# A four-layer graph network: node sums by (tile, block) visits held in PSUM, and waits by the group needed

## The reference

```python
# 1: two attention convolutions (with self loops): g = h @ W
e = leaky_relu(s[src] + d[dst]); alpha = softmax of e over the edges of dst
h = segment_sum(g[src] * alpha, dst) + bias
# 2: GCN (with self loops): dis = rsqrt(deg)
out = segment_sum((x @ W)[src] * dis[src] * edge_weight * dis[dst], dst) + b
# 3: relational attention, with a time mask sigmoid((t[dst] - edge_time) / |coeff|), 8 heads
out = segment_sum(v * attn, dst)
# 4: GGN: agg = segment_sum((h @ W_msg)[src], dst); a GRU cell of agg and h; @ W_out
x = layernorm(x + layer(x))          # after each of the four
```

## Time and profile before

| | us |
|---|---|
| median of three runs | 6013.23 (6009.44 to 6026.37) |
| profiled execution | 6018.44 |
| its span, first to last instruction | 6016.5 |
| busy: PE, PEld, DVE, ACT, POOL | 3699.8, 3070.5, 3610.2, 1531.2, 4144.0 |

### The profile page before, as it was taken

One profiled execution on the slowest core, in us unless ns is written; L12 is line 12 of the kernel. 1 busy time (PEld: TensorE's weight loads), 2 busy tenths in 40 slices (PEclk: granted clock), 3 DMA queues, 4 the chain that ended last, 5 costly groups with the idle time before them and its releaser, 6 DMA issues. The chain is left out here.

```text
span 6016.5 us, 106908 instructions
## 1 busy us (share of the span) xinstructions
PE 3699.8 (61%) x29332; PEld 3070.5 (51%) x29332; DVE 3610.2 (60%) x10962; ACT 1531.2 (25%) x3918; POOL 4144.0 (69%) x4416
## 2 busy tenths in 40 slices
PE   4765355566364344445555799999975864444556
PEld 2555355455353333445554577777754753344444
DVE  4699475699573235444554788888869952223235
ACT  0476000377100011000000455555540140000004
POOL 6677777377777746777776577777773447777772
PEclk8655698655596555555555899999987985555557
DMA  5687576488585544566772466666663732221221
GB/s 164 179 242 229 159 247 214 132 242 241 160 247 173 151 122 139 165 175 183 189 197 55 142 207 206 206 207 207 207 148 113 205 85 53 53 53 51 53 53 37
DMA packets 564739, 946.34 MB, mean 157 GB/s; under 512 B 122022, under 2 KB 225983, under 8 KB 563599
## 3 DMA queue, kind: packets, MB, share of 16 engines
q0 software_dynamic: 140576, 316.92, 21.1%
q1 hardware_dynamic: 263907, 405.95, 21.0%
q10 hardware_dynamic: 159712, 216.63, 11.7%
HBM read 705.34 MB, written 235.74 MB: 156 GB/s over the span
## 5 line engine op out<-in xcount | busy, mean ns | idle before, releaser
L256 POOL DMA_INDIRECT s_rows<-rel_tab,src_v x832 | 809.6, 973 | 272.5 <-issue 246.7
L256 POOL DMA_INDIRECT stash<-gat_tab,src_g x784 | 780.6, 996 | 251.8 <-issue 238.0
L256 POOL DMA_INDIRECT gcn_rows<-gcn_tab,src_g x784 | 751.9, 959 | 247.9 <-issue 236.2
L256 POOL DMA_INDIRECT ggn_rows<-ggn_tab,src_g x784 | 747.7, 954 | 248.3 <-issue 248.0
L256 POOL DMA_INDIRECT stash<-in_x,src_g x736 | 738.9, 1004 | 236.9 <-issue 223.1
L1595 PE MATMUL e_psb<-tmp,e_oh 128*128 x3328 | 553.4, 328 | 554.9 <-DVE e_oh L1566 459.3
L1595 PEld LDWEIGHTS e_psb<-tmp,e_oh 128*128 128x128 f32 x3328 | 495.7, 231 | 612.9 <-issue 612.8
L2108 PE MATMUL gcn_pso<-gcn_rows,gcn_oh 128*128 x1952 | 500.9, 438 | 484.1 <-SPq L965 396.4
L1940 PE MATMUL ggn_pso<-ggn_rows,ggn_oh 128*128 x1952 | 470.0, 417 | 492.2 <-SPq L965 486.1
L2108 PEld LDWEIGHTS gcn_pso<-gcn_rows,gcn_oh 128*128 128x128 f32 x1952 | 431.2, 325 | 510.2 <-issue 510.2
L1940 PEld LDWEIGHTS ggn_pso<-ggn_rows,ggn_oh 128*128 128x128 f32 x1952 | 405.8, 308 | 557.0 <-issue 557.0
(11 more groups left out here) (502 smaller groups left out, 8071.9 us busy)
## 6 DMA issues: line engine op xcount, KB each, us to landing
edge_v<-stash SPq DMA_DIRECT2D x392, 256.0 KB, 2.2
g_lo_rows<-lo_rows ACTq DMA_DIRECT2D x392, 256.0 KB
e_values<-edge_v SPq DMA_DIRECT2D x392, 256.0 KB, 4.2
oh_dram<-tmp ACTq DMA_DIRECT2D x208, 256.0 KB
s_oh<-oh_dram SPq DMA_DIRECT2D x208, 256.0 KB
edge_v<-acc SPq DMA_DIRECT2D x208, 256.0 KB
r_values<-edge_v SPq DMA_DIRECT2D x208, 256.0 KB, 3.0
tmp<-drel_rows ACTq DMA_DIRECT2D x208, 128.0 KB
```

The lines of the kernel that those rows point to most:

```text
L256: pool.indirect_dma_start(rows[:, t, :], None, tab[:, :], bass.IndirectOffsetOnAxis(ap=edges[:, t:t + 1], axis=0)).then_inc(s_land, 16)
```

## The change

Visits by (group, block) and all their tables are gone (`edge_rows`, `dst_tab`, `w_tab`, `grp_row`, `blk_row`, `slot_row`, `done_row`, L408 and the chain to `gvi`). `grow` is loaded straight from the inputs by nine DMAs, and half of the weight loads move from ACT's to SP's queue, ahead of the kept stores. GCN and GGN use the 832 (tile, block) visits in 208 iterations; sums stay in PSUM (four banks in GCN, eight in GGN), preset with `acc` by PE (identity matmul) for the first blocks and by ACT for later ones, and taken out by ACT. POOL itself announces landed groups, each behind the gathers of the next group; there are 16 slots. A new row `need_row` holds for each iteration the number of groups that must be there; PE waits for that count in GCN, GGN and `gat_sums`. In `gat_sums` DVE builds one-hots ten iterations ahead of the weighted values, with a ring of 14. In GGN the four one-hots of an iteration are one TENSOR_TENSOR instead of four TENSOR_SCALAR. In GCN the one-hots stay four TENSOR_SCALAR (from `drel_v` and `tm_v`), the DMAs of the static part move from ACT to SP, DVE instead of ACT takes the time products out of PSUM, and the three additions and Tanh come after the last iteration.

```diff
-V = GROUPS + BLOCKS - 1
...
-SLOTS = 14
+LEAD = 10
+AHEAD = LEAD + 4
+FEW = 4
...
-                    for a, name in enumerate(("dst", "src", "edge_type_64", "edge_weight")):
-                        arr = A[name] if a < 3 else A[name].bitcast(I32)
-                        sp.dma_start(edge_rows[0:FULL, a * GE:(a + 1) * GE],
...
+                    sp.wait_ge(s_pad, 3)
+                    for a, arr in enumerate((A["dst"], A["src"], A["edge_weight"].bitcast(I32))):
+                        sp.dma_start(grow[:, 0, a, :], arr[0:HALF_G * GE].rearrange("(g e) -> g e", e=GE)).then_inc(s_dl, 16)
+                        sp.dma_start(grow[0:FULL - HALF_G, 1, a, :], arr[HALF_G * GE:FULL * GE].rearrange("(g e) -> g e", e=GE)).then_inc(s_dl, 16)
+                        sp.dma_start(grow[FULL - HALF_G:HALF_G, 1, a, 0:REST], row(arr[FULL * GE:E])).then_inc(s_dl, 16)
+                    for g in range(EARLY, KEPT_FIRST):
+                        edges_of(g)
...
-                    sp.dma_start(grow[:, :, :], edge_rows[:, :].rearrange("(c p) e -> p c e", c=2)).then_inc(s_dl, 16)
-                    for g in range(EARLY, KEPT_FIRST):
-                        edges_of(g)
+                    weights(sp, later)
...
-                    for g in range(EARLY):
-                        gather_early(g)
-                    pool.wait_ge(s_gv, 1)
-                    for c in range(VC):
-                        pool.indirect_dma_start(er[:, c, :, :].rearrange("p a e -> p (a e)"), None, edge_rows[:, :],
-                                                bass.IndirectOffsetOnAxis(ap=gvi[:, c:c + 1], axis=0)).then_inc(s_er, 16)
-                    for g in range(EARLY, KEPT_FIRST):
+                    for g in range(KEPT_FIRST):
                         gather_early(g)
...
+                    link(v.tensor_scalar(need_row[:, :].unsqueeze(2), tile_i[:, :].rearrange("o (n t) -> o n t", t=GT)[:, :, GT - 1:GT], 2, None, ALU.arith_shift_right))
+                    link(v.tensor_scalar(need_row[:, :], need_row[:, :], 1, None, ALU.add))
...
-        def gather_rows(pool, rows, tab, s_row, s_used):
+        def ring_gathers(pool, rows, tab, s_row, s_in, s_o):
+            def came(g):
+                pool.wait_ge(s_row[g % WSLOTS], (g // WSLOTS + 1) * (16 * GT))
+                pool.sem_inc(s_in, 1)
             for g in range(GROUPS):
-                k = g % SLOTS
-                if g >= SLOTS:
-                    n = pool.value_load(done_row[0:1, g - SLOTS:g - SLOTS + 1], min_val=1, max_val=V)
-                    pool.wait_ge(s_used, n + RING)
+                if g >= WSLOTS:
+                    pool.wait_ge(s_o, GT * (g - 3))
                 pool.sem_inc(s_turn, 1)
-                gather_group(pool, rows[:, k, :, :], tab, src_g[:, g * GT:(g + 1) * GT], s_row[k])
-        def announce(sp, s_row, s_landed):
-            for g in range(GROUPS):
-                sp.wait_ge(s_row[g % SLOTS], (g // SLOTS + 1) * (16 * GT))
-                sp.sem_inc(s_landed, 1)
+                k = g % WSLOTS
+                gather_group(pool, rows[:, k * GT:(k + 1) * GT, :], tab, src_g[:, g * GT:(g + 1) * GT], s_row[k])
+                if g >= 1:
+                    came(g - 1)
+            came(GROUPS - 1)
+        def preset(act, ps_b, count, b, s_ev):
+            nc.scalar.activation(ps_b[:, b % count, 0:D], acc[:, b * D:(b + 1) * D], ACT.Copy).then_inc(s_ev, 1)
+        def evict(act, ps_b, count, b, s_o, s_tk, s_ev):
+            n = act.value_load(ends_row[0:1, b:b + 1], min_val=1, max_val=VT)
+            act.wait_ge(s_o, n)
+            nc.scalar.activation(acc[:, b * D:(b + 1) * D], ps_b[:, b % count, 0:D], ACT.Copy).then_inc(s_tk, 1)
+            if b + count < BLOCKS:
+                act.wait_ge(s_tk, b + 1)
+                preset(act, ps_b, count, b + count, s_ev)
+        def ring_sums(pe, ps_b, count, bank_of, oh, rows, s_in, s_oh, s_ev, s_o, beside=None):
+            its = count // GT
+            for b in range(count):
+                nc.tensor.matmul(ps_b[:, b, 0:D], ident[:, :], acc[:, b * D:(b + 1) * D], start=True, stop=True).then_inc(s_ev, 1)
+            for n in range(ITERS):
+                if n % its == 0:
+                    here = slice(n * GT, (n + its) * GT)
+                    blocks = several(mybir.EngineType.PE, blkv_row[0:1, here], BLOCKS - 1) if beside is not None else None
+                    newest = pe.value_load(blkv_row[0:1, here.stop - 1:here.stop], min_val=0, max_val=BLOCKS - 1)
+                    banks = several(mybir.EngineType.PE, bank_of[0:1, here], count - 1)
+                    slots = several(mybir.EngineType.PE, wslot_row[0:1, here], WSLOTS * GT - 1)
+                need = pe.value_load(need_row[0:1, n:n + 1], min_val=1, max_val=GROUPS)
+                pe.wait_ge(s_oh, n + 1)
+                if n % its == 0:
+                    pe.wait_ge(s_ev, newest + 1)
+                pe.wait_ge(s_in, need)
+                for t in range(GT):
+                    bank, slot = banks[n % its * GT + t], slots[n % its * GT + t]
+                    nc.tensor.matmul(ps_b[:, bass.ds(bank, 1), 0:D].rearrange("p o d -> p (o d)"), oh[:, n % RING, t, :],
+                                     rows[:, bass.ds(slot, 1), :].rearrange("p o d -> p (o d)"),
+                                     start=False, stop=True, skip_group_check=True).then_inc(s_o, 1)
+                if beside is not None:
+                    beside(n, blocks)
...
-                        def step(i, k):
-                            n = i * WSLOTS + k
-                            if n >= RING:
-                                dve.wait_ge(s_o, i * (WSLOTS * GT) + (k + 1 - RING) * GT)
-                            if n < GROUPS:
-                                dve.wait_ge(s_val[k % LOADED], i * (WSLOTS // LOADED * 16) + (k // LOADED + 1) * 16)
-                                w = gx[:, :, bass.ds(n * GT, GT)]
-                                v.tensor_copy(wv4[:, k, :, D:WCOLS], w.rearrange("p h t -> p t h"))
-                                v.tensor_tensor(wv4[:, k, :, 0:D], vr[:, k % LOADED, :, :], w[:, 0, :].unsqueeze(2).to_broadcast([P, GT, D]), ALU.mult)
-                            v.tensor_tensor(oh[:, k % RING, :, :], iota[:, :].unsqueeze(1).to_broadcast([P, GT, P]),
-                                            drel_v[:, bass.ds(n * GT, GT)].unsqueeze(2).to_broadcast([P, GT, P]), ALU.is_equal).then_inc(s_wv, 1)
+                        def weighted(g):
+                            if g >= WSLOTS:
+                                dve.wait_ge(s_o, GT * (g - 3))
+                            k = g % WSLOTS
+                            dve.wait_ge(s_val[g % LOADED], g // LOADED * 16 + 16)
+                            w = gx[:, :, g * GT:(g + 1) * GT]
+                            v.tensor_copy(wv4[:, k, :, D:WCOLS], w.rearrange("p h t -> p t h"))
+                            v.tensor_tensor(wv4[:, k, :, 0:D], vr[:, g % LOADED, :, :], w[:, 0, :].unsqueeze(2).to_broadcast([P, GT, D]), ALU.mult).then_inc(s_wv, 1)
+                        def onehots(n):
+                            if n >= AHEAD:
+                                dve.wait_ge(s_o, GT * (n + 1 - AHEAD))
+                            v.tensor_tensor(oh[:, n % AHEAD, :, :], iota[:, :].unsqueeze(1).to_broadcast([P, GT, P]),
+                                            drel_v[:, n * GT:(n + 1) * GT].unsqueeze(2).to_broadcast([P, GT, P]), ALU.is_equal).then_inc(s_oh, 1)
...
-                        for k in range(WSLOTS):
-                            step(0, k)
-                        for i in range(1, GROUPS // WSLOTS):
-                            for k in range(WSLOTS):
-                                step(i, k)
-                        for k in range(WSLOTS):
-                            step(GROUPS // WSLOTS, k)
+                        for n in range(LEAD):
+                            onehots(n)
+                        for g in range(GROUPS):
+                            weighted(g)
+                            if g + LEAD < ITERS:
+                                onehots(g + LEAD)
+                        for n in range(GROUPS + LEAD, ITERS):
+                            onehots(n)
...
+                            need = pe.value_load(need_row[0:1, n:n + 1], min_val=1, max_val=GROUPS)
+                            pe.wait_ge(s_oh, n + 1)
+                            if n % 2 == 0:
+                                pe.wait_ge(s_ev, newest + 1)
+                            pe.wait_ge(s_wv, need)
...
-                                i = v_.tensor_scalar(oh[:, k % 2, t, :], iota[:, :], dst_tab[:, col_], None, ALU.is_equal)
+                        v.memset(acc[:, :], 0.0).then_inc(s_z, 1)
+                        for n in range(ITERS):
+                            if n >= RING:
+                                dve.wait_ge(s_o, (n + 1 - RING) * GT)
+                            v.tensor_tensor(oh[:, n % RING, :, :], iota[:, :].unsqueeze(1).to_broadcast([P, GT, P]),
```

(24 more changed lines are left out.)

447 lines of the change are left out of this document (125 added, 322 removed).

## The result

The changed kernel takes 6253.76 us (median of four runs, 6242.55 to 6255.64) against 6014.9 us, a ratio of 1.0391 with a 95% interval of 1.0371 to 1.0410: slower by 239 us. 6046 us was forecast. The direction was right and the size was not; the range ended at 6072.

A forecast was written before the change was run, and what follows sets the result against it. POOL's indirect gathers, one every 1.25 us, were taken as the bound. 6018.4 - 15 (preparation) - 28 (attention sums) + 2 (GCN body) + 7 (GCN end) + 67 (GGN body) = 6051.4, 6046 us for the median; range 5980 to 6072.

The forecast's parts named there:

- What bounds the kernel: Whole kernel: POOL's row of indirect gathers bounds it, one starting every 1.25 us, 4960 of 6016.5 us; PE waits for gathers.
- Sums of both attention layers: Ends of both attention layers: need_row leaves two or three iterations behind the last weights, not 13; -28 us (-34 to -20).
- PE's clock or load being the bound after all: Rival on the visits: their rework shows by itself because PE is the bound; chance under 0.05, not priced apart.
- GGN body: GGN's one-hots: each TENSOR_TENSOR starts 0.20 us ahead of a group's fourth gather, stretching it 0.35 us; +67 us (45 to 85).
- Preparation: First phase: dropping the gvi chain and two gathers ends it at 76 us, with a 5 us stall; -15 us (-19 to -7).
- GCN body: GCN's iterations and POOL's landing waits: nearly all lies beside 5.0 us per group; +2 us (0 to 10).
- GCN end: Behind GCN's last iteration: additions, table load and Tanh no longer run beside gathers; +7 us (5 to 9).
- POOL would not starve on landings: GCN: landing waits cost nothing within a group's 5.0 us; the rival, POOL starving, had +30 us, 6076 us, chance 0.06.
- Sum: Whole kernel: all terms added to the profiled run give 6051.4 us, or 6046 us for the median.

The follow-up runs named there:

- e9: Changed kernel, but in the attention sums PE loads need_row only from iteration 160 on and waits for the constant n + 1 before: 6095.5 us.
- e14: Kernel of e9 with GGN's TENSOR_TENSOR one-hot 0.85 us earlier, in a ring of five buffers: 6044.8 us (1.0045).
- e13: Changed kernel with need_row loaded from iteration 160 on, GGN's one-hots as four TENSOR_SCALAR, and nothing large ahead of the stores on SP's preparation queue: 6022.8 us (1.0018).
- e15: Changed kernel, but in the attention sums PE loads one need_row value for two iterations, that of the later one: 6150.9 us (1.0231).
- e10: Changed kernel with need_row from iteration 160 on, a MEMSET before each GGN one-hot, edge numbers ahead of grow, weight loads back on ACT: 6097.5 us.
- e1: Changed kernel, but in the attention sums PE waits for the constant min(n + 1, 196), without need_row loads: 7992.0 us against 7947.7 for the kernel before.
- e2: The kernel of e9 on a chip where the kernel before takes 7947.7 us: 8016.6 us (1.0081).

## Why the prediction was right or wrong

**What bounds the kernel.** The 5.0 us for each group was right for GCN and GGN and was carried to the attention sums without a look at a stretch there. The earlier trace rows show only GCN and GGN. The same view at 820 to 920 us, quoted above, has the clock at 0.95 and weighted groups 1.8 us apart. On that row hangs the larger part of the error, 170 of the 208 us between 6046 and 6253.8; most of the rest is the preparation, 31.

**Sums of both attention layers** (forecast -28). This is the step that failed. It weighed the wait's meaning (a group needed earlier) and the one-hots, and gave the register load that carries the wait no term at all. The load stands on PE's sequencer 416 times, of which some 180 in the first and 120 in the second layer are iterations that PE works off without waiting for gathers. It lengthened such an iteration by 0.75 us, 0.2 of them idle time of PE and 0.55 the loss of the upper clock. The gain itself was there: in e9, with the load from iteration 160 on, the four stretches of both layers add to 2181.8 us against 2205.8 before, -24. Four iterations were left behind the last weights, not two or three. In the changed kernel only the second layer shows it (the finishing operations 20.8 us behind the last gather, not 34.5), as the first layer's PE is behind until its end (44.1 us). The list of rivals had "PE's clock or load being the bound after all" at under 0.05, argued from the earlier trace rows again.

**GGN body** (forecast +67, measured +54, range 45 to 85). Right, mechanism and place: the fourth gather of a group (mean 1206 ns, the other three 946 to 990) is held up by the one-hot, and e14 removes it by moving the one-hot. The held gathers add to 49 us; some 6 more are a gather of 7.8 us at the stage's start. Of the chain, one link was off: from the group's end to PE's weight load it takes 1.88 us (median of 160 groups; 1.93 in the group below), not 1.73, with POOL instead of SP passing the landing on.

```profile
5503.67 0.94 POOL L250 DMA_INDIRECT ggn_rows<-ggn_tab,src_g  x1 [0.30 <-issue]
...
5506.54 1.78 PEld L899 LDWEIGHTS ggn_psb<-ggn_rows,ggn_oh 128*128 128x128 f32 x8 [3.22 <-issue]
```

So the distance was 0.05 us in the median and not 0.20, at the very edge: 110 gathers were held up, 100 of them fourth ones of the 196 groups, by 0.48 us in the median, instead of nearly every fourth one by 0.35. The product came out near the forecast partly by luck. The Trainium skill infers on its page "SBUF — State Buffer", section "Who interferes with whom", that a tensor_tensor leaves the writing of DMA descriptors alone. The inference doesn't hold here: with the TENSOR_TENSOR 0.06 us ahead, the gather takes 1.45 us. The rule of the Trainium skill's same section that a tensor_tensor with both inputs in SBUF contends with GpSimd's reads would fit, as the gather takes its row numbers (src_g) from SBUF; no run tells the two apart. The Trainium skill says there too that a tensor_scalar in a 2-port mode blocks GpSimd. With four TENSOR_SCALAR the fourth gathers have a mean of 951 ns (e13, without one of 7.1 us) and none but that one is over 1.02 us; in which mode these ran, no view tells. That the later one waits until the earlier ends, which the same section says, agrees with the held gathers, which end at a fixed 0.81 to 0.83 us behind the one-hot.

**Preparation** (forecast -15, measured +16). The term named the right queue and sized it wrongly. It counted nine loads of grow at about 0.5 us of issue each. Two of them, small ones of 0.6 KB, held SP for 22.5 and 15.2 us, each behind two of 196 and 194 KB:

```profile
8.06 22.50 SPq L321 DMA_DIRECT2D grow<-in_src  x1
...
32.74 15.20 SPq L321 DMA_DIRECT2D grow<-in_edge_weight  x1
47.98 11.94 SPq L313 DMA_DIRECT2D p_early_edges<-in_src  x7
```

So not only the store of group 0 came late, as forecast, but the edge numbers of group 5, and POOL idled 24.7 us. The earlier trace rows had the hint: seven loads of 2 KB took 21.57 us to issue. Even without any stall (e13) the phase doesn't end before 90 us. The earliest end of 70.7 us counted the gathers and not the queues: in e13 ACT's is busy until 84.1 us and SP's until 88.6. Whether another order of the loads ends sooner wasn't tried.

**GCN body** (+2, measured +8) and **GCN end** (+7, measured +6). The scaling of tm_v starts 13.1 us behind the start of the last gather (13 to 14 forecast). Of the body's 8 us, 6 are the mean gather (966 against 959 ns) and 2 pauses on POOL; that POOL would not starve on landings held. 126 gathers instead of 76 are over 0.96 us; what lengthens them wasn't tried apart.

**Sum.** With -24 for -28, +54 for +67, +14 for +9 and the preparation as it came, the forecast's mechanisms would have given about 6075 us. Of the missing 180 us, 170 are the load of need_row (stretches of the attention layers, after against e9; 158 in total times), and 6 lie in the relational layer and behind GGN's last gather, for which there was no term.

## What to carry to other kernels

A wait that is more exact isn't free when its value has to be fetched: before a register load is put into a loop, find the stretches in which that engine is the bound, and look at each kind of stretch by itself, its clock included. Load such values where they matter (here from iteration 160 on); one load for two iterations still cost a little over half. A vector instruction that is triggered at a fixed distance from a gather meets the same gather every time; work out the distance, and move the trigger by a visit or two if it falls just ahead of a start.

## What the runs showed of the hardware

- A register load between matmuls with computed addresses cost the clock more than the time that it took: with one in every iteration of eight records the granted clock was 0.71 and PE idled 0.91 us an iteration, with half as many 0.79 and 0.85, with none 0.97 and 0.71 to 0.74 (first layer, after, e15, before and e9).
- An indirect gather was held up by a TENSOR_TENSOR 128x512 that began 0.047 to 0.5 us ahead of it; the gather then ended 0.81 to 0.83 us behind that instruction's end. A TENSOR_TENSOR that began 0.044 us ahead or less, or behind it, left the gather at 0.94 us. The edge is 0.003 us wide (changed kernel). With a MEMSET ahead of the TENSOR_TENSOR the edge lay 0.01 us behind the gather's start (e10).
- Three DMAs into 98 partitions behind each other, of 196, 194 and 0.6 KB, kept their queue for up to 22.5 us, all of it at the third and smallest.
- Three chips took 7948 to 8068 us for a kernel that takes 6015 elsewhere, with engines idle for nothing that the profile shows and POOL pausing mostly 2 to 7 us about every 30 gathers in GGN. On one of them e1 (7992.0 us) stood ahead of e2 (8016.6), against what was expected; e1 wasn't run elsewhere.
